# Five small operations on a token's two shares move from DVE to GpSimd

## The reference, cut to what matters

```
x = x + agent_attention(group_norm(x))              # 8 heads, 16 agents, 5 masks
t = tokens(x)
t = t + linear_attention(layer_norm(t))             # softmax-free, elu(q)+1, elu(k)+1
t = t + mixture(layer_norm(t))                      # 8 experts, the best 2 per token
# in mixture, per token:
logits = x @ router_w + router_b                    # 8 numbers
top_w, sel = top_k(logits, 2); top_w = softmax(top_w)
out = sum over the two experts of top_w * expert(x)
```

## Time and profile before

| | |
|---|---|
| median of 3 runs | 1207.85 us |
| the profiled execution: its time, its span | 1216.59 us, 1214.8 us |
| busy over the span | PE 85%, DVE 73%, PEld 71%, ACT 59%, POOL 48% |
| `agent_attention`, about | 0 to 377 us |
| `token_mixer`, about | 377 to 764 us |
| `experts`, about | 764 to 1215 us |

### The profile page before, as it was taken

The page is one execution under the profiler, slowest core; times in us unless marked ns, Lnnn a source line. Parts: engine busy times, 40 slices in busy tenths (PEclk is TensorE's granted clock), DMA queues, the critical chain, the costliest instruction groups (busy, mean ns, idle before and its releaser), DMA issues. The chain is left out here.

```text
span 1214.8 us, 39840 instructions
## 1 busy us (share of the span) xinstructions
PE 1034.6 (85%) x12967; PEld 857.2 (71%) x12968; DVE 891.0 (73%) x2181; ACT 714.4 (59%) x1446; POOL 583.1 (48%) x630
## 2 busy tenths in 40 slices
PE   5799999999986887888887840699999999999995
PEld 4477877787763456666666740588888898888984
DVE  5687777777773347877877762488888888888985
ACT  1277665666643257676676620567676767676763
POOL 0425746374676215555655552144444444444443
PEclk9899999999997778999999965799999999999998
DMA  8011101011103001111211219221112111221110
GB/s 308 26 38 28 38 21 35 21 37 29 29 3 105 18 18 41 59 58 59 68 51 60 65 56 142 55 57 50 52 55 56 51 52 48 56 56 52 35 23 1
DMA packets 72324, 64.18 MB, mean 53 GB/s; under 512 B 9812, under 2 KB 58227, under 8 KB 72237
## 3 DMA queue, kind: packets, MB, share of 16 engines
q1 hardware_dynamic: 57132, 43.46, 13.3%
q0 software_dynamic: 10016, 17.16, 4.6%
q10 hardware_dynamic: 5090, 2.32, 1.5%
HBM read 33.44 MB, written 24.72 MB: 48 GB/s over the span
## 5 line engine op out<-in xcount | busy, mean ns | idle before, releaser
L1318 POOL DMA_INDIRECT out<-e_y,e_xg x184 | 183.7, 998 | 77.8 <-issue 77.6
L1366 PE MATMUL e_ps<-e_xt,w_hl 128*128 128x256 f16 x736 | 202.2, 275 | 14.2 <-issue 12.8
L1367 PE MATMUL e_ps<-e_xt,w_hl 128*128 128x256 f16 x736 | 201.8, 274 | 0.0
L1368 PE MATMUL e_ps<-e_xt,w_hl 128*128 128x256 f16 x736 | 201.7, 274 | 0.0
L810 POOL DMA_INDIRECT rows<-m_rows,m_place x128 | 127.5, 996 | 44.4 <-issue 44.4
L251 POOL TENSOR_SCALAR vm<-v,early 128x512 f32<-128x512 f32 x96 | 148.5, 1562 | 0.0
L1383 PE MATMUL e_ps<-w_hl,e_hid_hl 128*128 x736 | 145.6, 220 | 0.0
L1384 PE MATMUL e_ps<-w_hl,e_hid_hl 128*128 x736 | 144.9, 219 | 0.0
L1382 PE MATMUL e_ps<-w_hl,e_hid_hl 128*128 x736 | 144.1, 220 | 0.0
L1443 DVE SCALAR_TENSOR_TENSOR e_hid_hl<-e_hid,e_hid_hl 128x512 f16<-128x512 f32 x184 | 127.4, 692 | 20.0 <-ACT e_hid_hl L1416 19.7
L1437 DVE SCALAR_TENSOR_TENSOR e_hid<-e_ps,e_act 128x512 f32<-128x512 f32 x184 | 125.9, 684 | 15.2 <-ACT e_act L1422 10.9
(11 more groups left out here) (249 smaller groups left out, 2603.6 us busy)
## 6 DMA issues: line engine op xcount, KB each, us to landing
e_xg<-rows SPq DMA_DIRECT2D x92, 133.0 KB
resid<-in_x SPq DMA_DIRECT2D x8, 1024.0 KB, 13.9
xb<-in_x SPq DMA_DIRECT2D x32, 256.0 KB, 2.7
m_rows<-resid SPq DMA_DIRECT2D x32, 256.0 KB, 2.7
out<-e_y,e_xg POOLq DMA_INDIRECT x184, 2.3
m_w_f<-in_L_ffn_gate_up_proj SPq DMA_DIRECT2D x1, 2048.0 KB, 8.2
rows<-m_rows,m_place POOLq DMA_INDIRECT x128, 2.4
rows<-nobody SPq DMA_DIRECT2D x15, 133.0 KB, 10.0
```

The costliest lines, as they stand in the source:

```text
L1318: nc.gpsimd.indirect_dma_start(out_rows, bass.IndirectOffsetOnAxis(ap=who, axis=0), y[:, slot, i, :], None, bounds_check=B * TOK - 1, oob_ ...
L1366: t.matmul(o, hi, x2[0], start=True, stop=False)
L1367: t.matmul(o, hi, x2[1], start=False, stop=False)
L1368: last = t.matmul(o, lo, x2[0], start=False, stop=True)
```

## The change

Of the seven operations of `shares`, DVE keeps the first two (L1178 and L1179 before). The other five (L1180, L1181, L1182, L1184, L1185) become a function `shares` on POOL, at the end of its list as `(2, shares)`, which is behind `power` and ahead of the `ring_power` of the next body. POOL waits in it for the reciprocal on DVE (semaphore `place_step`), counts its own five steps on a new semaphore `share_step`, and `rows_ready` waits for them too. DVE waits for `share_step` of the pair before in `route` and `shares`, because the same small tile `best` is overwritten there.

```
+            def shares(k, ring):
+                slot = 2 * ring
+                one, two, more, share = (best[:, n, :] for n in (6, 7, 11, 3))
+                step = chain(pool, s.share_step, SHARE_STEPS * k)
+                pool.wait_ge(s.place_step, PLACE_STEPS * k + 2)
+                step(g.tensor_tensor(two, share, one, ALU.mult))
+                step(g.tensor_tensor(more, one, two, ALU.subtract))
+                step(g.tensor_tensor(more, more, best[:, 9, :], ALU.mult))
+                need(pool, s.rows_out, SENT * (k - 1))
+                step(g.tensor_tensor(rows[:, slot:slot + 2, :, WLO], w3(two), w3(more), ALU.add), False)
+                step(g.tensor_tensor(rows[:, slot:slot + 2, :, WHI], w3(one), w3(more), ALU.subtract), False)
...
+                pool.wait_ge(s.share_step, SHARE_STEPS * (k + 1))
...
             pipelined(pool, PAIRS, 4, 2, [
-                (0, ring_power), (3, rows_ready), (3, send, 0), (3, send, 1), (0, biases_low), (1, power),
+                (0, ring_power), (3, rows_ready), (3, send, 0), (3, send, 1), (0, biases_low), (1, power), (2, shares),
             ])
...
             def shares(k, ring):
-                slot = 2 * ring
                 step = chain(dve, s.place_step, PLACE_STEPS * k)
                 need(dve, s.ew_done, k + 1)
-                one, two, more = (best[:, n, :] for n in (6, 7, 11))
-                step(v.tensor_scalar(two, best[:, 3, :], WS, WS, ALU.mult, ALU.add))
-                step(v.reciprocal(one, two))
-                step(v.tensor_tensor(two, best[:, 3, :], one, ALU.mult))
-                step(v.tensor_tensor(more, one, two, ALU.subtract))
-                step(v.tensor_tensor(more, more, best[:, 9, :], ALU.mult))
-                need(dve, s.rows_out, SENT * (k - 1))
-                step(v.tensor_tensor(rows[:, slot:slot + 2, :, WLO], w3(two), w3(more), ALU.add), False)
-                step(v.tensor_tensor(rows[:, slot:slot + 2, :, WHI], w3(one), w3(more), ALU.subtract), False)
+                need(dve, s.share_step, SHARE_STEPS * k)
+                step(v.tensor_scalar(best[:, 7, :], best[:, 3, :], WS, WS, ALU.mult, ALU.add))
+                step(v.reciprocal(best[:, 6, :], best[:, 7, :]), False)
```

More of the change, by code:

```diff
@@ L44 @@
 ROW = C + 5
-LN_STEPS, ROUTE_STEPS, EXP_STEP, PLACE_STEPS, COLUMN_STEP = 7, 14, 9, 10, 26
+SHARE_STEPS, LN_STEPS, ROUTE_STEPS, EXP_STEP, PLACE_STEPS, COLUMN_STEP = 5, 7, 14, 9, 5, 26
 WALL = 3 * C + E
@@ L710, in token_mixer @@
             s_psum kv_done o_psum mix_step add_done norm2 xT2 xt2_done lg_psum route ew_done meta_done
-            rank_psum place_step place_done held rows_out table nobody_set nobody_in res0_in res1_in col_psum""".split()})
+            rank_psum place_step share_step place_done held rows_out table nobody_set nobody_in res0_in res1_in col_psum""".split()})
         res_in = [s.res0_in, s.res1_in]
         b2_row = b2_hl[:].rearrange("p e c -> p (e c)")
+        w3 = lambda ap: ap.rearrange("p (u j) -> p u j", u=2)
         def tails(eng, first):
@@ L1168, in route @@
                 step(v.tensor_tensor(oh16[:], wide(best[:, 8, :], G), pair, ALU.is_equal), False)
-            w3 = lambda ap: ap.rearrange("p (u j) -> p u j", u=2)
             def shares(k, ring):
-                slot = 2 * ring
                 step = chain(dve, s.place_step, PLACE_STEPS * k)
                 need(dve, s.ew_done, k + 1)
-                one, two, more = (best[:, n, :] for n in (6, 7, 11))
-                step(v.tensor_scalar(two, best[:, 3, :], WS, WS, ALU.mult, ALU.add))
-                step(v.reciprocal(one, two))
-                step(v.tensor_tensor(two, best[:, 3, :], one, ALU.mult))
-                step(v.tensor_tensor(more, one, two, ALU.subtract))
-                step(v.tensor_tensor(more, more, best[:, 9, :], ALU.mult))
-                need(dve, s.rows_out, SENT * (k - 1))
-                step(v.tensor_tensor(rows[:, slot:slot + 2, :, WLO], w3(two), w3(more), ALU.add), False)
-                step(v.tensor_tensor(rows[:, slot:slot + 2, :, WHI], w3(one), w3(more), ALU.subtract), False)
+                need(dve, s.share_step, SHARE_STEPS * k)
+                step(v.tensor_scalar(best[:, 7, :], best[:, 3, :], WS, WS, ALU.mult, ALU.add))
+                step(v.reciprocal(best[:, 6, :], best[:, 7, :]), False)
             def placed(k, ring):
                 slot = 2 * ring
-                step = chain(dve, s.place_step, PLACE_STEPS * k + 7)
+                step = chain(dve, s.place_step, PLACE_STEPS * k + 2)
                 need(dve, s.rank_psum, k + 1)
```

## The result

The changed kernel took 1220.99 us (median of 4 runs, 1220.30 to 1222.22); the kernel before took 1207.09 us beside it (4 runs, 1205.22 to 1208.79). The ratio is 1.0117, with an interval of 1.0098 to 1.0135: slower by 13.9 us, where +18.7 us was forecast. A second series gave 1.0133 (1.0115 to 1.0152).

What follows compares the result with a forecast made beforehand. The order of waits was taken as the bound, DVE setting the pace and handing work to and fro with PE. Delay 9.3 less 0.6 at the end, plus 10 for the clock, on 1207.85 gave 1226 us; range 1213 to 1239.

Steps and rivals of the forecast that it cites:

- The mechanism: Loop from body to body: reciprocal (DVE), five operations and `ring_power` (POOL), `norm1` (ACT), `xT` and `outs` (PE), then DVE; +18.7 us.
- The 1.2 us of slack: On POOL before the change: `ring_power` ends 1.20 us before ACT's `norm1`, which needs it, starts.
- POOL's chain: From the reciprocal's end through five share operations to `ring_power` done on POOL: 1.60 us.
- the rival of the doubled cost: GpSimd operations cost double, 7.7 us more in all, and the clock falls each time: 1246 us; chance 0.03.
- The way from there: From `ring_power` through `norm1` and `xT` to `outs`: waits of 0.05 and 0.06 us, `outs` 3.99 us behind the reciprocal.
- The delay per body: `outs` starts 0.73 us later in six odd bodies and 0.98 in five even ones, bodies 5 to 15: 9.3 us.
- The end: After body 15 no `ring_power` follows, so the operations removed from DVE give back 0.6 us.
- The clock: PE's longer wait, in five even bodies, lets TensorE's clock fall, at 2.0 us each: +10 us.
- The three cases of the earlier trace: PE waits of 2.56 and 2.97 us in bodies 3 and 4 preceded a lower clock; 2.17 in body 16 did not.
- The delay alone: Rival: PE idles 2.07 to 2.43 us but the clock holds, 1216.6 us; chance 0.24.
- The gain: Rival: shares fit into POOL's and ACT's slack, `outs` 0.59 us earlier in 13 bodies, 1199.6 us; chance 0.06.
- The signs: Profile after: later `ring_power`, new waits of `norm1` and `xT`, longer DVE wait, reciprocals 18.6 to 18.9 us apart, clock near 0.9.

Runs made afterwards that it cites:

- e1_behind_ring: The changed kernel with the five moved operations put behind `ring_power` of the next body on POOL; 1201.65 us, ratio to before 0.9933.
- e2_wait_last: The kernel before with only a POOL wait for the seventh operation on DVE added in the place of the change; 1230.92 us, ratio 1.0167.
- e2_wait_recip: The kernel before with only a POOL wait for the reciprocal on DVE added in the place of the change; 1209.21 us, ratio 0.9998.
- e3_longer: The changed kernel with the first of the five share operations on POOL done five times; 1245.57 us, ratio 1.0314.
- the filled kernel: The changed kernel with 24 unused products of constants on PE between `sums` and `xT` from body 3 on; 1213.28 us, ratio 1.0032.

## Why the prediction was right, and where it was off

**The mechanism** came out as told: `ring_power` became a link of a loop through all four engines. `e1_behind_ring` and `e2_wait_last` show it from both sides: the work without the place gains, the place without the work loses. The 1.2 us of slack that the prediction names are only those ahead of `norm1`. In `e2_wait_recip` `ring_power` came 2.67 us later at no cost, since `xT` had slack ahead of `outs`, too; in the changed kernel it comes 3.51 us later. The prediction's sum compares at `outs` and so has this right.

**POOL's chain.** 1.60 us from the reciprocal's end was forecast, 1.46 came (531.85 to 533.31): 0.08 to the first operation, 0.28 for each dependent one, 0.16 for the independent. The Trainium skill (GPSIMD Engine Reference, section Engine selection) has GpSimd about twice as slow with two inputs. That does not hold at 128x8, by these rows: the moved operations take 0.20 to 0.21 us where DVE took 0.17. So the rival of the doubled cost falls.

**The way from there.** ACT starts 0.21 us after `ring_power` ends (0.05 forecast), and `xT` 0.13 after `norm1` (0.06). With POOL's 0.14 to the good that makes `outs` 4.13 us behind the reciprocal instead of 3.99. An even body adds 0.21 us of issue at the branch, not 0.36: 554.56 - 550.15 = 4.41, forecast 4.35.

**The delay per body.** A body without a drop of the clock takes 18.50 (odd) and 18.82 (even, twice in the second profile): +0.65 and +0.97, forecast 0.73 and 0.98. Over the eleven bodies that is 6 x 18.50 + 5 x 18.82 - 11 x 17.85 = 8.75 us, where 9.3 was forecast. The body is a little shorter than the later `outs` would have it: its rest, from L1155 to the reciprocal, takes 13.24 us instead of 13.36.

**The end.** The last two intervals take 27.63 us instead of 28.04: 0.41 given back, 0.6 forecast. `picked` follows the reciprocal there by 0.50 us instead of 1.10, but not all of it reaches the end.

**The clock is the term that was mis-sized, twice.** The step read "I take it that the longer one, of the even bodies, lets the clock fall and the shorter does not", at 2.0 us each in five bodies: +10. First, there is no line between 2.07 and 2.43 us. Behind the same wait of 2.17 us odd bodies lost the clock (5, 11, 15) or held it (7, 9, 13) in one execution, and others did so in the next; even bodies, behind 2.44, lost it five times of five and then three of five. What the runs show is a chance that is higher behind longer waits of `xT`. Of bodies 5 to 15, one of 11 lost the clock behind 1.33 to 2.06 us (`e2_wait_recip`), 7 of 12 behind 2.17 and 8 of 10 behind 2.44 in the two profiles of the changed kernel, and all 11 behind 3.29 to 3.58 (`e3_longer`). The Trainium skill (TensorE: Matmul & The Clock Gate, section Part 1: The HAM clock gate) says that the count of products at the lower level at the start of a kernel varies from run to run of the same kernel. The two profiles show the like in the steady stretch, with 8 bodies and 7, four of them the same. The three cases of the earlier trace rows should have been read as draws, not as a limit.

Second, the price was taken from body 4, where `xT` and `outs` ran at the lower level from start to end (1.11 and 2.18 us). Over the whole of body 4 the granted clock was 0.84. In the bodies of the changed kernel that lost it, it was 0.91 or 0.92, which is about half as much time at the lower level; in body 8 `xT` still takes 0.68, and the clock falls behind it. A drop costs (213.04 - 205.1) / 8 = 1.0 us, with 205.1 = 6 x 18.50 + 5 x 18.82. Eight at 1.0 is 7.9 against five at 2.0, so the two errors nearly cancelled: that the whole term came near its size was luck.

**What the sum left out.** Before had two drops of its own in bodies 7 and 15 (18.62 and 18.75, together 1.67 us above 17.85). I added new drops to a body of 17.85 and took nothing off for these. By terms, for bodies 5 to the end: 8.75 + 7.9 - 1.67 - 0.41 = 14.6 us.

It also put bodies 3 and 4 at zero. The chain is hidden there, as told (`norm1` starts 2.36 us after the first reciprocal in both kernels), but the removed operations gain: in body 3 `outs` waited 0.92 us for `keys_values` before, and starts 5.12 us after the reciprocal now instead of 5.62. The clock was higher, too. Bodies 3 and 4 of before, then of the changed kernel (columns as in the earlier trace rows):

```profile
455.57:477.69 22.12, 17.43 (x107) 14.18 (x105) 16.68 (x56) 15.18 (x34) 11.03 (x13) 0.85 0.16 49
477.69:499.30 21.61, 17.20 (x107) 14.04 (x105) 16.78 (x55) 15.36 (x34) 11.94 (x13) 0.84 0.17 51
...
451.56:471.72 20.16, 16.20 (x107) 13.19 (x105) 15.99 (x51) 15.05 (x33) 12.78 (x18) 0.92 0.17 54
471.72:492.43 20.71, 16.03 (x107) 13.32 (x105) 16.00 (x51) 14.85 (x32) 12.95 (x18) 0.92 0.18 53
```

That is 40.87 us instead of 43.73, 2.86 less; the second profiles have 40.81 and 43.95. With it the terms give 11.7 us, which is what the two profiles show from the first reciprocal to the last. Between the medians it is 13.9. Both profiled executions of before lie above its median (1216.59 and 1210.75 us), so an ordinary run may have less to gain in these bodies; where the other 2 us lie is not shown.

**The rivals.** The delay alone would have been 1216.6 us, and the filled kernel, where the clock mostly holds, comes near it: 1.0032 x 1207.09 = 1210.9. Its bodies 3 and 4 take 38.85 us, 4.9 less than before in the profiles; without that it would be 1215.8. The gain came where its condition holds, in `e1_behind_ring`: -0.67% is 8.1 us, and the rival had -8.3. In its parts it is off: 0.52 per loop body instead of 0.59, and in the profiles 2.83 in bodies 3 and 4 (40.90 us) instead of 1.2.

**The signs.** `ring_power` 1.44 us after the reciprocal's start (told as about 1.6), `norm1` waiting 2.41 (2.4), `xT` 2.17 and 2.44 (2.1 to 2.4), DVE 2.74 (2.7). The clock over the steady stretch was 0.94 (below 0.98, near 0.9). Wrong was "over 20 where the clock fell": mostly 19.4 to 19.8, and over 20 in one body of each profile.

## What to carry to other kernels

Before work goes to an engine that looks idle, look for what stands behind it in that engine's queue, and how much slack the most hurried of its customers has, followed to the place where the engines meet. Here a `ring_power` 2.67 us later cost nothing, one 3.51 us later cost 1.2%, and moving one entry of a list turned that into -0.7%. A new wait on PE of some 2 us is to be priced twice, as a delay and as a chance of a lower clock; in these runs the second was a chance per body, higher behind longer waits. Where such a wait can't be avoided, products of constants in it can give back most of the clock, as they did here, though not the delay.

## What was not expected of the hardware

- At one and the same wait of PE, 2.17 us, the granted clock fell in some bodies and not in others, and in different ones from one execution to the next, for about 1.0 us each time.
- A wait put ahead of `ring_power` in POOL's loop let it start 0.40 us behind the event in most odd bodies and 0.65 in most even ones; in body 3, which is written out, it was 0.08, as with a wait that the operation carries. What takes the rest in the loop is not shown.
- Two operations on POOL of 0.21 us each took 1.80 and 0.92 us where they fell beside operations of 1.75 and 0.95 us on DVE (`e3_longer`, bodies 3 and 4), and ended 0.07 to 0.08 us after them. That they waited for DVE is likely, but was not tried.
- The kernel before gains 0.24% (0.12 to 0.36) from 24 products in each body whose results nobody reads.
- One operation of the statistics on DVE (L1055 before, 128x8) takes 0.16 to 0.29 us before, and 0.16 to 0.17 after the change (15 each). In body 9 of before the 0.29 fell beside POOL's last indirect transfer (583.63 to 584.59, the operation at 584.27); after the change POOL was idle there. It makes up the 0.12 us by which the rest of an odd body became shorter. In `e1_behind_ring` the same body has a transfer there again (576.00 to 576.96), and the operation, at 576.59, takes 0.35. That the transfer is the cause was not tried by itself.
